# Layernorms moved ahead of the last down product, attention weights by casting DMAs: a macaron block on eight cores

## What is computed

```python
# x: (1, 16384, 2048) f32; gate_w, up_w: (8192, 2048) int32; down_w: (2048, 8192) int32
def ffn(h):
    g = h @ ((gate_w - 128.) * gate_scale[:, None]).T
    u = h @ ((up_w - 128.) * up_scale[:, None]).T
    return (silu(g) * u) @ ((down_w - 128.) * down_scale[:, None]).T

def attn(h):                       # 32 heads of 64 in 4 groups of 8
    q = (h @ Wq + bq).reshape(B, L, 4, 8, 64)
    kv = (h @ Wkv + bkv).reshape(B, L, 4, 2, 64)
    scores = einsum('blghd,blgd->blgh', q, k)[..., None] / 8
    return (softmax(scores, axis=-1) * v[:, :, :, None, :]).reshape(B, L, 2048)

x = x + 0.5 * ffn(layernorm(x))
x = x + attn(layernorm(x))
x = x + 0.5 * ffn(layernorm(x))
```

## Time and profile before

| | us |
|---|---|
| median of 4 runs | 7582.35 |
| the 4 runs | 7803.45, 7361.26, 7358.7, 7929.44 |
| the profiled execution | 7362.25 |
| its span on the slowest core (core 2) | 7360.7 |
| spans of the 8 cores | 7337.6 to 7360.7 |

### The profile page before, as it was taken

One profiled execution on the slowest core, in us unless ns is written; L12 is line 12 of the kernel. 1 busy time (PEld: TensorE's weight loads), 2 busy tenths in 40 slices (PEclk: granted clock), 3 DMA queues, 4 the chain that ended last, 5 costly groups with the idle time before them and its releaser, 6 DMA issues.

```text
span 7360.7 us, 64221 instructions; the slowest of 8 cores (7337.6 to 7360.7 us)
## 1 busy us (share of the span) xinstructions
PE 5961.5 (81%) x26650; PEld 2690.3 (37%) x26650; DVE 973.2 (13%) x1040; ACT 874.5 (12%) x654; POOL 237.3 (3%) x340
## 2 busy tenths in 40 slices
PE   1898689967699889984356389979997499979997
PEld 1443234423344334431223144434443244334432
DVE  1100000000300000001344420000000200000000
ACT  1333113320200000000101110000000200000000
POOL 0000100010000000000000000000000000000000
PEclk9999899989799999997687689999998799999998
DMA  7566766586222542256121422263225322352235
GB/s 149 202 232 213 219 199 232 200 261 149 90 78 72 140 123 75 72 140 178 65 52 40 83 75 75 89 143 103 78 86 143 103 78 75 114 146 76 76 112 134
DMA packets 273912, 914.53 MB, mean 124 GB/s; under 512 B 23380, under 2 KB 23508, under 8 KB 246741
## 3 DMA queue, kind: packets, MB, share of 16 engines
q1 hardware_dynamic: 218328, 675.51, 29.2%
q0 software_dynamic: 48384, 184.57, 11.2%
q10 hardware_dynamic: 6912, 50.33, 2.0%
HBM read 725.77 MB, written 201.33 MB: 126 GB/s over the span
## 4 chain that ended last, share of the span: by engine, by line
PE 68%; DMA 21%; DVE 5%; ACT 2%; issue 2%; another core or an unknown queue 1%; DVEq 0%; SPq 0%; ACTq 0%; POOL 0%; POOLq 0%
PE PS L418 48%; PE PS L541 13%; DMA WD<-dwb 10%; DMA xo<-ARF 5%; PE PS L657 3%; DMA dwb<-WD 2%; PE PS L328 2%; DVE ST L292 1%; DMA ARF<-dwt 1%; ACT ARF L316 1%; DVE ARF L562 1%; PE PS L632 1%; DVE YT L338 1%; ACT WD L493 1%
## 5 line engine op out<-in xcount | busy, mean ns | idle before, releaser
L541 PE MATMUL PS<-WD,ARB 128*128 128x512 bf16 x8192 | 1933.8, 393 | 487.9 <-DVE ARF L562 194.0
L418 PE MATMUL PS<-YT,WG 128*128 128x512 bf16 x8192 | 1823.0, 381 | 47.2 <-DVE ARF L562 42.5
L418 PE MATMUL PS<-YT,WU 128*128 128x512 bf16 x8192 | 1809.9, 379 | 0.0
L541 PEld LDWEIGHTS PS<-WD,ARB 128*128 128x128 bf16 x8192 | 794.3, 100 | 1627.4 <-issue 823.3
L418 PEld LDWEIGHTS PS<-YT,WG 128*128 128x128 bf16 x8192 | 804.4, 98 | 1024.5 <-issue 67.8
L418 PEld LDWEIGHTS PS<-YT,WU 128*128 128x128 bf16 x8192 | 801.2, 98 | 966.9
L439 DVE SCALAR_TENSOR_TENSOR ARB<-ARF,CON,PS 128x1024 bf16<-128x1024 f32 x256 | 327.7, 1280 | 3237.1 <-PE PS L418 3237.1
L432 ACT ACTIVATE ARF<-PS,CON 128x1024 f32<-128x1024 f32 x256 | 285.2, 1114 | 3847.4 <-PE PS L418 3847.3
L328 PE MATMUL PS<-CON,ARF 128*128 128x128 f32 x768 | 172.7, 419 | 524.9 <-ACT ARF L316 524.9
L562 DVE TENSOR_TENSOR ARF<-PS,ARF 128x1024 f32<-128x1024 f32 x128 | 156.8, 1225 | 2333.4 <-PE PS L541 2117.8
L328 PEld LDWEIGHTS PS<-CON,ARF 128*128 128x128 f32 x768 | 156.5, 226 | 545.2 <-issue 545.2
(11 more groups left out here) (38 smaller groups left out, 596.4 us busy)
## 6 DMA issues: line engine op xcount, KB each, us to landing
WD<-dwb SPq DMA_DIRECT2D x448, 512.0 KB, 3.7
WG<-gwb SPq DMA_DIRECT2D x192, 512.0 KB, 3.2
WU<-uwb SPq DMA_DIRECT2D x192, 512.0 KB, 3.2
ARB<-gwt SPq DMA_DIRECT2D x64, 1024.0 KB, 6.3
ARB<-uwt SPq DMA_DIRECT2D x64, 1024.0 KB, 9.4
ARF<-dwt SPq DMA_DIRECT2D x64, 1024.0 KB, 8.5
xo<-ARF POOLq DMA_DIRECT2D x128, 512.0 KB, 9.3
ARF<-xo ACTq DMA_DIRECT2D x48, 1024.0 KB, 4.8
```

Of the source, the lines that this page charges most:

```text
L418: wring=wring, soff=soff: E.matmul(dst[:, j * 512:j * 512 + w], wring[:, soff + k * 128: soff + (k + 1) * 128], yt[:, k * TILE + j * 512: ...
L541: tsv=tsv, ic=ic: E.matmul(psd[:, j * 512:j * 512 + w], arb[:, ic * TILE + tsv * 128: ic * TILE + tsv * 128 + 128], wd[:, soff + jj * D2 + ...
```

## The change

- `ln_stage` is called earlier for four phases: att0, att1, f2a and f2b. `ln_junction(tile)` is a callback: `ffn_phase` calls it in its second half, between the gate/up products and the down products; `attn_phase` calls it after the Q products, ahead of the softmax. The next phase takes the result with `take_pending_ln`. Junctions stand in f1b, att0, att1 and f2a. Only the layernorms of f1a and f1b remain at the head of their phase.
- The barriers at the end of the phases and the one after the last `bcast_row` go. Waits for single counters take their place (the accumulates, VectorE's last operation, the counters of PSUM's readers).
- Wq and Wkv are no longer loaded as f32 and cast by VectorE. Casting DMAs of GpSimd's queue write bf16 into `ARB`. `preload_B`, ahead of f1b, loads Wkv and 4 of the 16 pieces of Wq into the part of `ARB` above the hidden activations; `load_A`, at the head of att0, loads the other 12 pieces, once the down products no longer read the hidden activations.
- The places in `ARB` are reckoned anew; KV's results lie at its start.
- VectorE's wait for `dpe` stands once per half. Marks and named scopes label the program.

```diff
-        ARB_FFN = ICH * TILE + 8 * D
-        ARB_ATT = KC * D + KC * KVW + 2 * NSUB * KVW
-        ARB_N = max(ARB_FFN, ARB_ATT)
+        RB = ICH * TILE
+        WKVB2 = RB
+        _curB = RB + KC * KVW
+        _capB = RB + 8 * D
+        if 2 * NSUB * KVW <= RB:
+            _kvs_off = 0
+            _curA = 2 * NSUB * KVW
+        for k in range(KC - 1, -1, -1):
+            if _curB + D <= _capB:
+                WQ_OFFS[k] = _curB
+                _curB += D
+            elif _curA + D <= RB:
+                WQ_OFFS[k] = _curA
+                _curA += D
...
         def bcast_row(drow, width, ps_off, dst_off, scale):
             b.wait("sync", "pbc", b.n("pbc"))
+            for sl in range(3):
+                b.wait("sync", f"gac{sl}", b.n(f"gac{sl}"))
+            prevv = b.last_done.get("vector")
+            if prevv is not None:
+                b.wait("sync", prevv[0], prevv[1])
...
-        def ln_stage(tile, scalar_first_waits=()):
+        def ln_stage(tile, extra_waits=()):
+            prevln = b.aux.get("ln_prev")
...
+            prevv = b.last_done.get("vector")
+            if prevv is not None:
+                b.wait("scalar", prevv[0], prevv[1])
+            for sl in range(3):
+                b.wait("scalar", f"gac{sl}", b.n(f"gac{sl}"))
+            for sl in range(2):
+                b.wait("scalar", f"aac{sl}", b.n(f"aac{sl}"))
             b.psum_fence("tensor")
...
-        def ffn_phase(tile, is_int):
-            sfw = []
-            yT_ready = ln_stage(tile, scalar_first_waits=sfw)
-            ln_ptr_final = b.n("ptr")
+        def ln_junction(tile):
+            def j():
+                extra = [("scalar", "vhh", b.n("vhh"))]
+                v = ln_stage(tile, extra_waits=extra)
+                b.aux["pending_ln"] = (tile, v)
+            return j
...
+        def ffn_phase(tile, is_int, junction=None):
+            b.mark("ln")
+            yT_ready = take_pending_ln(tile)
+            if yT_ready is None:
+                yT_ready = ln_stage(tile)
+            ln_ptr_final = b.aux["ln_prev"]["ptr"]
...
                             if ic < 2:
-                                b.wait("tensor", "vfl", flush_base_prev_half)
+                                for s in ("vfl", "vqb", "vkv", "vbc"):
+                                    b.wait("tensor", s, b.n(s))
+                                b.wait("tensor", "vte", b.n("vte"))
...
-                    b.wait("vector", "dpe", b.aux.get("half_dpe", 0))
+                    if ic == 0:
+                        b.wait("vector", "dpe", b.aux.get("half_dpe", 0))
+                        b.wait("vector", "pq", b.n("pq"))
...
+                if half == 1 and junction is not None:
+                    b.mark("junc")
+                    junction()
...
                             if first_group and ch == 0:
                                 b.wait("tensor", "vhh", hh_done)
+                                b.wait("tensor", "vte", b.n("vte"))
...
-            for sl in range(3):
-                b.wait("gpsimd", f"gac{sl}", b.n(f"gac{sl}"))
-            b.barrier()
...
+        def preload_B():
+            for s in ("gdq", "udq", "ddq"):
+                b.wait("gpsimd", s, b.n(s))
+            for s in ("gil0", "gil1", "uil0", "uil1", "dil0", "dil1"):
+                b.wait("gpsimd", s, b.n(s))
+            for k in range(KC):
+                b.op("gpsimd", lambda E, k=k: E.dma_start(
+                    out=arb[:, WKVB2 + k * KVW:WKVB2 + (k + 1) * KVW],
+                    in_=d_wkv[k * 128:(k + 1) * 128, :]),
+                    incs=[("qlb", 16)], dma=True)
+            for k in range(KC):
+                if WQ_OFFS[k] >= RB:
+                    b.op("gpsimd", lambda E, k=k: E.dma_start(
+                        out=arb[:, wq_off(k):wq_off(k) + D],
+                        in_=d_wq[k * 128:(k + 1) * 128, :]),
+                        incs=[("qlb", 16)], dma=True)
+
+        def load_A():
+            b.wait("gpsimd", "dpe", b.n("dpe"))
+            b.wait("gpsimd", "vhh", b.n("vhh"))
+            for k in range(KC):
+                if WQ_OFFS[k] < RB:
+                    b.op("gpsimd", lambda E, k=k: E.dma_start(
+                        out=arb[:, wq_off(k):wq_off(k) + D],
+                        in_=d_wq[k * 128:(k + 1) * 128, :]),
+                        incs=[("qla", 16)], dma=True)
...
             if first:
-                for k in range(KC):
-                    xsoff = XS0 if (k % 2) == 0 else XS1
...
-                b.wait("sync", "vqc", b.n("vqc"))
+                load_A()
+                b.wait("sync", "voa", b.n("voa"))
                 bcast_row(d_bq, D, 0, DSBC, None)
                 bcast_row(d_bkv, KVW, 2048, BKVB, None)
...
+            b.wait("vector", "dpe", b.n("dpe"))
             for ts in range(NSUB):
...
                 if ts == 0:
                     b.wait("tensor", "vte", yT_ready)
+                    b.wait("tensor", "qlb", b.n("qlb"))
...
+            b.wait("vector", "sy", b.n("sy"))
+            for sl in range(2):
+                b.wait("vector", f"aac{sl}", b.n(f"aac{sl}"))
             for ts in range(NSUB):
...
                     b.wait("tensor", "vkv", b.n("vkv"))
+                    if ts == 0:
+                        b.wait("tensor", "qla", b.n("qla"))
...
+            if junction is not None:
+                b.mark("junc")
+                junction()
+
             SALL = TMP
...
-            for sl in range(2):
-                b.wait("gpsimd", f"aac{sl}", b.n(f"aac{sl}"))
-            b.barrier()
...
-        ffn_phase(1, is_int=False)
-        attn_phase(0, first=True)
-        attn_phase(1, first=False)
+        preload_B()
+        ffn_phase(1, is_int=False, junction=ln_junction(0))
+        attn_phase(0, first=True, junction=ln_junction(1))
+        attn_phase(1, first=False, junction=ln_junction(0))
         b.wait("sync", "voa", b.n("voa"))
         bcast_row(d_dsr, D, 0, DSBC, 0.5)
-        b.barrier()
-        ffn_phase(0, is_int=False)
+        ffn_phase(0, is_int=False, junction=ln_junction(1))
         ffn_phase(1, is_int=False)
```

More of the change, by code:

```diff
@@ L283, in ln_stage @@
                     b.wait("scalar", "ptr", base["ptr"] + NBAT * (ts - 1))
+                elif prevln is not None:
+                    b.wait("scalar", "sy", prevln["sy"])
+                    b.wait("scalar", "vrs", prevln["vrs"])
+                    b.wait("scalar", "ptr", prevln["ptr"])
                 b.op("scalar", lambda E, xs=xs, r0=r0: E.dma_start(
@@ L589, in attn_phase @@
+        def load_A():
[7 more added lines that the diff above has]
+                        incs=[("qla", 16)], dma=True)
+        def attn_phase(tile, first, junction=None):
             BKVB = TMP + D + KVW
@@ L603, in attn_phase @@
-                for k in range(KC):
-                    b.wait("sync", "vqc", b.n("vqc"))
[L605 to L608, removed]
-                    b.wait("vector", f"qld{k % 2}", b.n(f"qld{k % 2}"))
-                    b.op("vector", lambda E, k=k: E.tensor_copy(
-                        arb[:, WKVB + k * KVW:WKVB + (k + 1) * KVW],
-                        arf[:, TMP:TMP + KVW]), incs=[("vqc", 1)])
@@ L613, in attn_phase @@
-                b.wait("sync", "vqc", b.n("vqc"))
+                load_A()
+                b.wait("sync", "voa", b.n("voa"))
                 bcast_row(d_bq, D, 0, DSBC, None)
                 bcast_row(d_bkv, KVW, 2048, BKVB, None)
-            yT_ready = ln_stage(tile, scalar_first_waits=(
-                [("scalar", "vqc", b.n("vqc"))] if first else []))
+            b.mark("aln")
+            yT_ready = take_pending_ln(tile)
+            if yT_ready is None:
+                yT_ready = ln_stage(tile)
@@ L740, in build_program @@
         b.wait("vector", "vbc", b.n("vbc"))
+        b.mark("f1a")
         ffn_phase(0, is_int=True)
@@ L743, in build_program @@
             b.wait("sync", s, b.n(s))
-        ffn_phase(1, is_int=False)
-        attn_phase(0, first=True)
-        attn_phase(1, first=False)
+        b.mark("f1b")
+        preload_B()
+        ffn_phase(1, is_int=False, junction=ln_junction(0))
+        b.mark("att0")
+        attn_phase(0, first=True, junction=ln_junction(1))
+        b.mark("att1")
+        attn_phase(1, first=False, junction=ln_junction(0))
         b.wait("sync", "voa", b.n("voa"))
         bcast_row(d_dsr, D, 0, DSBC, 0.5)
-        b.barrier()
-        ffn_phase(0, is_int=False)
+        b.mark("f2a")
+        ffn_phase(0, is_int=False, junction=ln_junction(1))
+        b.mark("f2b")
         ffn_phase(1, is_int=False)
+        b.mark("tail")
         for sl in range(3):
             b.wait("gpsimd", f"gac{sl}", b.n(f"gac{sl}"))
+        for sl in range(2):
+            b.wait("gpsimd", f"aac{sl}", b.n(f"aac{sl}"))
+        segs = []
+        prev = ("init", {e: 0 for e in ENGS})
+        for name, pos in b.marks + [("end", {e: len(b.ops[e]) for e in ENGS})]:
+            segs.append((prev[0], prev[1], pos))
```

(11 more changed lines are left out.)

64 lines of the change are left out of this document (41 added, 23 removed).

## The result

| | before | after |
|---|---|---|
| executions compared, us | 7358.7, 7361.26, 7364.9 | 7231.15, 7249.09, 7257.45 |
| ratio, 95% interval | 1 | 0.9843 (0.9813 to 0.9873) |
| the same, a second time on another chip | 1 | 0.9859 (0.984 to 0.9879) |
| mean span of the 8 cores, profiled execution | 7352.2 | 7233.0 |
| slowest core of it | 7360.7 | 7253.1 |

The median of all seven executions of the changed kernel is 7496.19 us (before: 7783.22 of ten), outside the predicted range of 7203 to 7285, because in many of them one or both dies ran part of the time at a lower clock; all comparisons here leave those executions out. In the others the change takes 1.4 to 1.6% off, some 104 to 116 us. The prediction was 1.8%, 131.7 us. It had the sign, the rough size and the mechanism right, and several terms of its sum wrong.

What follows compares the result with a forecast made beforehand. TensorE was taken to bound the kernel, standing idle at the seams around bare layernorms. Savings of 102.5 + 16.4 + 12.0 + 13.3 less 12.5 make 131.7 us, so 7362.25 falls to about 7230 us, range 7203 to 7285.

Steps and rivals of the forecast that it cites:

- the layernorm is not laid over matmuls: Between gate/up and down: a moved layernorm still costs its 98 us, 100.0 in all with wait and load issue.
- the casting loads are hidden: First FFN to attention: twelve late Wq pieces take 45 us at 280 GB/s, within 58.4 us; seam saves 102.5 us.
- The argument by streams read and written: Casting loads: an accumulate reads two streams per one written, a cast one, so about 320 GB/s; 280 taken.
- the accumulate's 162 GB/s: Low end for the cast rate, from GpSimd's accumulating DMAs: late Wq pieces take 78 us, Q starts 19 us late.
- rival 1: Casting loads are slow: 7258 us at 162 GB/s, 7348 at 81; range 7247 to 7350, chance 0.19.
- KV's second tile waiting for VectorE: Inside attention, a sign of being right: second tile's KV waits about 45 us on VectorE, busy with softmax and outputs.
- Q to Q: First layernorm inside attention, first tile's Q to second's: 16.4 us saved, the last output DMA's landing and two KV units.
- three meet it: First FFN, tile 0 to 1: three x loads meet the early casting loads, 4.2 us more each, 12.5 us lost.
- X loads of over 9 us: Tile 1's first layernorm, a sign of being wrong: x loads over 9 us, or more than three meeting casting loads.
- the two small loads run beside the Wq loads, for which I take 3 us: Entry to attention: bias-row loads crowded by Wq loads cost 3 us (0 to 8), rows 21.6 us in all.
- at nothing: List of items counted as zero: VectorE's dpe wait, waits at stage starts, scopes, and TensorE restarts (5 us either way).
- then ds is loaded and spread, 12.4 us: Attention to second FFN: down scale row takes 12.4 us plus 0.4 before gate/up; the seam saves 12.0 us.

Runs made afterwards that it cites:

- run 6: Changed kernel with bias rows bq and bkv spread by two repeated-source loads into WG and WU, ds row not reloaded; ratio 0.9783 to the kernel before.
- run 3: Changed kernel with the old weight loads: Wq and Wkv as f32 at att0's head, cast by VectorE; ratio 0.9978 to the kernel before.
- run 10: Changed kernel without ScalarE's new wait for VectorE's last operation in the very first layernorm; first gate/up starts at 217.1 us, 220.8 with the wait.
- run 1: Changed kernel without its four junctions, every layernorm at its phase's head, casting loads and missing barriers kept; ratio 0.9893 to the kernel before.
- run 2: Changed kernel with only att0's layernorm back at the head of its phase, three junctions left; ratio 0.987 to the kernel before.
- run 7: Changed kernel with x prefetched and the next subtile's statistics and normalization ahead of this one's transposes and copies; ratio 0.9647 to the kernel before.
- run 4: Changed kernel with the 20 early casting loads issued behind tile 1's first layernorm instead of ahead of it; 7239.23 and 7242.35 us.

## Where the prediction held and where it failed

**Held.** That the layernorm is not laid over matmuls: 100.8 us in the junction against the 100.0 reckoned. That the casting loads are hidden: 45 us against 45, and run 6 showed 46 us in the open. The argument by streams read and written had given 320 GB/s, the rows of the plain load 280; the rows were right. That the accumulate's 162 GB/s is no measure for a cast: rival 1 is out. KV's second tile waiting for VectorE, in the changed kernel 42.71 us against the 45 announced:

```profile
3873.47 22.35 PE L716 MATMUL PS<-ARB,YT 128*128 128x512 bf16 x94 [42.71 <-DVE ARB L724]
```

and Q to Q 17.3 saved against 16.4.

**Near by luck: the early casting loads.** The step "three meet it", at 4.2 us each, 12.5 us, had both factors wrong. Two of the x loads met them, 11.64 and 11.37 us long instead of 4.81, so 6.8 and 6.6 us longer; the second costs only some 5, because it used to end before VectorE was ready for it. The layernorm took 12.0 us more for these two on core 2, and the stretch on the mean 10.5. X loads of over 9 us had been named as a sign of being wrong, and it came. The Trainium skill (DMA: Bandwidth & Descriptors, Anatomy of one DMA — SWDGE path), with 2.0 us a DMA plus its bytes at 436 GB/s, stood in the prediction for two x loads and 8.4 us. The trace agrees in the number of loads and not in the rate: the 12.6 MB of the twelve later loads, read in 45 us, are 280 GB/s.

**Failed: terms mis-sized, all of one kind,** the price of transfers and waits that now meet each other. The step "the two small loads run beside the Wq loads, for which I take 3 us": the rows took 26.5 us, not 21.6. In run 3, where nothing runs beside them, they took from 3632.59 to 3650.43, 17.8, on core 2:

```profile
3632.59 0.25 SPq L268 DMA_DIRECT2D ARF<-bq_r  x1
3634.51 0.17 DVE L271 MEMSET ARF<- 1x128 f32 x1 [2.01 <-DMA ARF<-bq_r]
...
3649.74 0.69 DVE L287 COPY ARF<-PS 128x512 f32<-128x512 f32 x1 [2.89 <-PE PS L279]
```

So crowding costs 8.7, beyond the upper end of my 0 to 8. With the accumulate's landing, 19.5 in place of 17.5 (the casting loads run beside that too), these are 6.9 of the 8.5 us missing at this seam on core 2 (94.0 saved, not 102.5); the layernorm and KV are the rest. On the mean of the cores 5.5 are missing.

The list of terms "at nothing" does not name ScalarE's new wait for VectorE's last operation, so the sum had it at nothing without a reason. It stands in `ln_stage`, so also in the first one, where VectorE still copies the down scale row. I looked for what is queued behind a new wait on its own engine and not for what another queue sends ahead meanwhile: 4.1 us, of which run 10 gets 3.7 back by taking the wait out. The same oversight made the expectations of runs 1 and 2 fall at the entry to attention.

The step "then ds is loaded and spread, 12.4 us" and 0.4 to gate/up: measured, core 2,

```profile
4165.23 0.22 SPq L268 DMA_DIRECT2D ARF<-ds_r  x1
4165.56 0.36 SPq L460 DMA_DIRECT2D WG<-gwb  x1
...
4169.92 0.17 DVE L271 MEMSET ARF<- 1x128 f32 x1 [5.01 <-DMA ARF<-ds_r]
...
4178.40 2.29 DVE L291 TENSOR_SCALAR ARF<-PS 128x2048 f32<-128x2048 f32 x1 [8.32 <-PE PS L279]
4181.33 8.02 PE L481 MATMUL PS<-YT,WG 128*128 128x512 bf16 x31 [3.10 <-DVE ARF L291]
```

16.1 us to gate/up, not 12.8. The row is used 4.7 us after its issue, in the kernel before 1.7 (4170.09 to 4171.80). Without the barrier SyncE issues gate/up's first four weight loads 0.3 us behind the 8 KB row, and the last output's DMA is issued at 4165.57; before, the row was alone. I take these 3 us for the removed barrier's price, read from the timeline and not tested by a run of its own; I had only priced its gain.

**From one core to eight.** I took the seams of core 2, the slowest, and the mean of the cores gave 118.9 us at the last matmul instead of 131.7. The choice of the core does not explain this. On core 2 the seams save 94.0 (entry to attention), 19.2, 8.3 and 12.7 us and lose 6.1 (start) and 13.0 (f1a to f1b): 115.1 together, against 118.1 on the mean. Only at the last seam does the choice matter: 13.3 predicted, 12.7 on core 2, 10.1 on the mean. The matmul blocks of core 2 then took 7.1 us longer than before, where the sum had nothing, and this leaves 108.1 at its last matmul. On the mean these blocks took 0.8 us less, and they do not repeat any better: on the mean of the cores they were 0.9 us shorter than before in run 7, 2.5 in run 4, 5.4 in run 10 and 13.5 in run 3.

Beyond that, the time is that of the slowest core. It lay 8.5 us above the mean of the spans before, and 20.1 in the profiled execution after (7253.1 against 7233.0). The blocks of down products differ from core to core by 10 to 17 us in both kernels; whether they add up differently by chance or because the barriers or the loads changed stays open. It is the remaining difference between 119 on the mean and 108 on the slowest core.

## What to carry to other kernels

Moving a serial stage to another place on the same in-order engines wins only what stood around it, here 2 to 17 us a seam by run 1. Look first at whether its own order is the chain: writing the statistics of the next subtile ahead of the copies of this one took 27 us off each of six layernorms. When a barrier goes, list what each queue will now send while the small transfer on the path is in flight. The other way round, price a new wait by what other queues get in ahead of the instruction behind it. Here the long transfers off the path could be sized from their bytes and the rate of a plain load; the 8 KB rows on the path could not, they took three times as long beside them.

## What the runs showed of the hardware

Casting DMAs from f32 to bf16 on GpSimd's queue ran at 273 to 280 GB/s of f32 read (12.6 MB in 45 to 46 us, twice), as fast as the plain f32 loads of the same tensor before (280 GB/s), and twelve issues of them took 6.66 us. An 8 KB load on SyncE's queue, which is used 1.9 us after its issue when nothing runs beside it (run 3), took 6.6 us beside them (3548.30 to 3554.86), and 4.7 us with four weight loads issued behind it. A 1 MB load of x took 11.4 to 11.6 us beside casting loads, and 4.8 without them.
